# A four-phase graph network on one core: own term from DRAM, a wait for each half, and the last layer written node by node

## The reference, cut to what matters

```python
h = relu(layernorm(x1))                              # x1: the result of the first network, [3125, 128]
h3 = relu(mean(h[src] by dst) @ W_l0.T + b_l0 + h @ W_r0.T)      # third phase,  [3125, 256]
h4 = relu(mean(h3[src] by dst) @ W_l1.T + b_l1 + h3 @ W_r1.T)    # fourth phase, [3125, 256]
h5 = relu(h4 @ W_lin1.T + b_lin1)                                # [3125, 256]
out = x1 + h5 @ W_lin2.T + b_lin2                                # [3125, 128]
```

## Time and profile before

| what | value |
|---|---|
| time, median of 3 runs | 600.82 us (600.31 to 601.1) |
| profiled execution, its own time | 599.37 us |
| span of the profiled execution | 597.6 us |
| PE busy | 554.2 us, 93% of the span |
| PEld / DVE / ACT busy | 294.3 / 218.6 / 215.9 us |
| mean granted TensorE clock | 1.000 |
| DMA | 22.99 MB, mean 38 GB/s |

### The profile page before, as it was taken

How to read it: one execution, slowest core, us unless ns; L and a number is a source line. 1 busy time by engine, 2 the same in 40 slices (tenths; PEclk the granted TensorE clock), 3 DMA queues, 4 the chain that set the end, 5 groups by cost and what they waited for, 6 DMA issues and landing times.

```text
span 597.6 us, 9565 instructions
## 1 busy us (share of the span) xinstructions
PE 554.2 (93%) x3131; PEld 294.3 (49%) x3131; DVE 218.6 (37%) x489; ACT 215.9 (36%) x391; POOL 24.0 (4%) x34
## 2 busy tenths in 40 slices
PE   1457999999999999999999999999999999999996
PEld 0244655555554654445455555544544445454454
DVE  6888968577774227667311111100100001010000
ACT  1588857577674204454432212101101110111021
POOL 4320000000000000101100000000000000000000
PEclk9999999999999999999999999999999999999999
DMA  3700103010010133332110000200110202010011
GB/s 94 190 2 1 37 1 114 2 35 17 17 34 18 23 90 97 94 103 54 40 29 18 17 17 5 93 21 0 21 32 1 50 0 51 0 38 13 6 33 28
DMA packets 27421, 22.99 MB, mean 38 GB/s; under 512 B 4143, under 2 KB 26928, under 8 KB 27264
## 3 DMA queue, kind: packets, MB, share of 16 engines
q1 hardware_dynamic: 25670, 21.45, 13.5%
q10 hardware_dynamic: 1561, 0.84, 0.5%
q0 software_dynamic: 160, 0.33, 0.3%
HBM read 16.42 MB, written 6.19 MB: 38 GB/s over the span
## 4 chain that ended last, share of the span: by engine, by line
PE 86%; DVE 5%; ACT 3%; DMA 2%; issue 2%; POOL 1%; ACTq 0%; DVEq 0%; SPq 0%; POOLq 0%
PE ps L1011 53%; PE ps L1028 23%; PE ps L965 5%; PE ps L1021 2%; DVE hs_b L473 1%; DMA adj<-key_d,adj 1%; ACT hs_b L774 1%; PE ps L1245 1%; ACT adj L1481 1%; DMA invc<-inv_d 1%; POOL adj L1357 1%; PE ps L1217 1%; POOL adj L1364 1%; DVE adj L1408 1%; PE ps L1291 1%
## 5 line engine op out<-in xcount | busy, mean ns | idle before, releaser
L1011 PE MATMUL ps<-adj,hs_b 125*128 (+2 forms) x1050 | 205.7, 351 | 0.0
L1011 PE MATMUL ps<-adj,hs_a 125*128 (+2 forms) x700 | 158.6, 353 | 0.0
L1011 PEld LDWEIGHTS ps<-adj,hs_b 125*128 125x128 f16 x1050 | 95.9, 97 | 105.4 <-issue 9.9
L473 DVE TENSOR_TENSOR hs_b<-iota,hs_b 128x1024 f16<-128x1024 f16 x150 | 95.9, 686 | 29.6 <-PE ps L965 28.0
L965 PE MATMUL ps<-hs_b 128*128 128x125 f16 x625 | 69.4, 235 | 21.4 <-DVE hs_b L473 13.4
L813 ACT ACTIVATE adj<-ps 125x500 f32 (+2 forms) x150 | 80.2, 543 | 23.6 <-PE ps L965 17.3
L965 PEld LDWEIGHTS ps<-hs_b 128*128 128x128 f16 x625 | 46.7, 104 | 67.2 <-DVE hs_b L473 34.7
L1011 PEld LDWEIGHTS ps<-adj,hs_a 125*128 125x128 f16 x700 | 58.6, 98 | 38.8 <-issue 5.4
L763 DVE TENSOR_TENSOR hs_a<-ps,hs_a 125x512 f32<-125x512 f32 (+1 forms) x7 | 4.4, 634 | 170.3 <-PE ps L1291 170.3
L1028 PE MATMUL ps<-aggT,wts 128*128 128x500 f32 (+1 forms) x112 | 44.6, 540 | 0.4 <-ACT aggT L924 0.4
L1028 PE MATMUL ps<-aggT,hs_a 128*128 128x500 f32 (+1 forms) x84 | 35.1, 540 | 0.5 <-ACT aggT L952 0.5
(11 more groups left out here) (152 smaller groups left out, 358.8 us busy)
## 6 DMA issues: line engine op xcount, KB each, us to landing
invc<-inv_d SPq DMA_DIRECT2D x24, 250.0 KB, 3.3
self_d<-hs_b SPq DMA_DIRECT2D x6, 250.0 KB, 2.0
hs_b<-self_d SPq DMA_DIRECT2D x6, 250.0 KB, 3.5
hs_b<-in_x_dram SPq DMA_DIRECT2D x6, 250.0 KB
x_d<-hs_b SPq DMA_DIRECT2D x6, 250.0 KB
hs_a<-x_d SPq DMA_DIRECT2D x6, 250.0 KB
out_dram<-hs_a SPq DMA_DIRECT2D x6, 250.0 KB
wt_d<-adj SPq DMA_DIRECT2D x1, 1152.0 KB, 4.2
```

The source lines that it names most:

```text
L473: last = nc.vector.tensor_tensor(onehots[slot], iota2.unsqueeze(1).to_broadcast(shape), keys[:, ds(g * 4, 4), :].unsqueeze(2).to_broadcast ...
L1011: last = nc.tensor.matmul(acc[:, 0:n], hs[:, ds(s * (2 * w) + part * w + h * 128, 128)], adj[0:P, ds(c * (S * C) + s * n, n)], start=(isin ...
```

## The change

Three parts, all about the fourth phase.

1. SP stores each chunk's ReLU output of the third phase (`actT`) to a new DRAM tensor `h3_d` (f32, 500 KB for a full chunk), and ACT waits for that store before it overwrites `actT`. In the fourth phase SP loads `h3T` from it; `own4` and its two ACT copies are gone.
2. In `staged` TensorE waits in front of tile 0 and tile 25, each time for the eviction of the half whose bank it is about to overwrite. Phase 3 keeps the wait it had.
3. `lin2` takes slices of 125 nodes of `aggT` as the stationary operand and the weights (128 columns) as the moving one, and so writes node by feature into bank 2. `turn4` and ACT's bias copy are gone. VectorE adds the bias row (`bbb`, loaded once to all partitions, in the place of `zT`) to x1, and then writes the sum from bank 2.

```diff
+        h3_d = nc.dram_tensor("h3_d", [128, 2 * N], F32, kind="Internal").ap().rearrange("p (m n) -> p m n", m=2)
+        bbb = zT[:, 0:D]
...
                     load_inv("p3_", c + 1, nxt)
+                n = width(full)
+                sp.wait_ge(sem("p3_relu"), 2 * c + 2)
+                sp.dma_start(h3_d[:, :, ds(c * C, n)],
+                             actT.rearrange("p (m n) -> p m n", m=2)[:, :, 0:n]).then_inc(sem("p3_h3_out"), 16)
...
             load_x1(0, True)
+            sp.dma_start(bbb, bb.partition_broadcast(128)).then_inc(sem("p4_bb"), 16)
+
+            def load_h3(c, full):
+                n = width(full)
+                sp.dma_start(wts[:, 0:2 * C].rearrange("p (m n) -> p m n", m=2)[:, :, 0:n],
+                             h3_d[:, :, ds(c * C, n)]).then_inc(sem("p4_h3"), 16)
+            sp.wait_ge(sem("p3_h3_out"), 16 * NCH)
+            sp.wait_ge(sem("p3_h3"), 2 * NCH)
+            load_h3(0, True)
 
             def step4(c, full, nxt):
                 sp.wait_ge(sem("p4_agg_out"), 2 * c + 2)
                 if nxt is not None:
                     load_inv("p4_", c + 1, nxt)
+                    sp.wait_ge(sem("p4_h4"), 2 * c + 2)
+                    load_h3(c + 1, nxt)
                 sp.wait_ge(sem("p4_sum"), c + 1)
...
-                dve.wait_ge(sem("p4_turned"), c + 1)
                 dve.wait_ge(sem("p4_x1"), 16 * c + 16)
+                dve.wait_ge(sem("p4_bb"), 16)
+                nc.vector.tensor_tensor(tiles(x1in[:, 0:nt * D], D), tiles(x1in[:, 0:nt * D], D),
+                                        bbb[0:P].unsqueeze(1).to_broadcast([P, nt, D]), ALU.add).then_inc(sem("p4_x1b"), 1)
+                dve.wait_ge(sem("p4_lin2"), c + 1)
+                dve.wait_ge(sem("p4_x1b"), c + 1)
                 wait_past(dve, "p4_out", 16 * c)
-                nc.vector.tensor_tensor(outb[:, 0:nt * D], bank(3, nt * D, P), x1in[:, 0:nt * D], ALU.add).then_inc(
+                nc.vector.tensor_tensor(outb[:, 0:nt * D], bank(2, nt * D, P), x1in[:, 0:nt * D], ALU.add).then_inc(
                     sem("p4_sum"), 1)
...
                 wait_past(act, "p3_turned", 2 * c)
+                wait_past(act, "p3_h3_out", 16 * c)
...
-                for m in range(2):
-                    act.wait_ge(sem("p4_own"), 2 * c + m + 1)
-                    if m == 0:
-                        wait_past(act, "p4_turned", c)
-                    nc.scalar.activation(h3T[:, m * C:m * C + n], bank(2 + m, n), ACT.Copy).then_inc(sem("p4_ownT"), 1)
...
-                act.wait_ge(sem("p4_lin2"), c + 1)
-                nc.scalar.activation(h3T[:, 0:n], bank(2, n), ACT.Identity, bias=bbc).then_inc(sem("p4_lin2T"), 1)
...
-                        if at == 0 and ph > 2 and not done:
-                            wait_past(pe, f"p{ph}_agg_out", len(aggs) * c)
+                        if at % S == 0 and ph > 2 and at >= done:
+                            wait_past(pe, f"p{ph}_agg_out", len(aggs) * (c - 1) + at // S + 1)
...
-            def own4(c, full):
-                wait_past(pe, "p4_lin2T", c)
-                own(hbz, H, 0, 2, c, full).then_inc(sem("p4_own"), 1)
-                wait_past(pe, "p4_sum", c)
-                own(hbz, H, 1, 3, c, full).then_inc(sem("p4_own"), 1)
...
-                pe.wait_ge(sem("p4_ownT"), 2 * c + 2)
+                pe.wait_ge(sem("p4_h3"), 16 * c + 16)
...
-                dense(2, n, [(bv[:, k, :], aggT[:, k * C:k * C + n]) for k in range(2)]).then_inc(sem("p4_lin2"), 1)
-
-            def turn4(c, full):
-                pe.wait_ge(sem("p4_lin2T"), c + 1)
-                for t in range(width(full) // P):
-                    last = nc.tensor.transpose(bank(3, 4 * D, P)[:, t * D:(t + 1) * D], h3T[:, t * P:(t + 1) * P], identf[:])
-                last.then_inc(sem("p4_turned"), 1)
+                wait_past(pe, "p4_sum", c)
+                for t in range(n // P):
+                    for k in range(2):
+                        last = nc.tensor.matmul(bank(2, 4 * D, P)[:, t * D:(t + 1) * D], aggT[:, k * C + t * P:k * C + (t + 1) * P],
+                                                bv[:, k, :], start=(k == 0), stop=(k == 1))
+                last.then_inc(sem("p4_lin2"), 1)
             staged(4, [(fixed(0), hbz, H, 0), (fixed(1), hbz, H, 1)],
-                   [(0, own4, 1), (10, hidden4, 1), (20, lin1, 1), (30, lin2, 1), (40, turn4, 1)],
+                   [(10, hidden4, 1), (20, lin1, 1), (30, lin2, 1)],
```

More of the change, by code:

```diff
@@ L934, in act_layers @@
             chunks(act, step3)
-            h3T = wts[:, 0:2 * C]
             def step4(c, full):
                 n = width(full)
-                for m in range(2):
-                    act.wait_ge(sem("p4_own"), 2 * c + m + 1)
-                    if m == 0:
-                        wait_past(act, "p4_turned", c)
-                    nc.scalar.activation(h3T[:, m * C:m * C + n], bank(2 + m, n), ACT.Copy).then_inc(sem("p4_ownT"), 1)
                 for m in range(2):
@@ L1297, in pe_layers @@
             if not slow:
-                for part in (own4, hidden4, lin1, lin2, turn4):
+                for part in (hidden4, lin1, lin2):
                     part(NFULL, False)
```

## The result

The changed kernel takes 590.86 us, the median of 4 runs (590.59 to 592.12), against 600.57 us for the kernel before on the same chip: a ratio of 0.9846, 95% interval 0.9827 to 0.9866, which is 8.0 to 10.4 us less. The forecast was 591.8 us, with 590.0 to 594.6. A second series on another occasion gave 591.02 us and 0.9849 (0.9836 to 0.9863).

A forecast was written before the change was run, and what follows sets the result against it. TensorE was taken to bound the kernel, busy 554.2 of 597.6 us. Own term 5.28, waits 0.66, last layer 2.02 and end 1.10 summed to 9.06 us, so 600.82 became 591.8 us, range 590.0 to 594.6.

The forecast's parts named there:

- What bounds the kernel: Until the last aggregation ends, an edit's price is the TensorE time taken out or put in; afterwards every step's latency counts.
- Own term and the two waits: Fourth-phase passes: removing own4 gains 0.88 us x 6 = 5.28 us; waiting per half gains 0.06 + 4 x 0.15 = 0.66 us.
- the bare eviction: Start of each pass: removing own4 without the finer waits would expose the second bank's eviction, some 0.7 us a pass.
- A satisfied wait in mid-stream: A wait already met inside the TensorE stream: taken at nothing, bounded by 0.15 us once or twice a pass.
- The last layer: lin2 as 16 instructions takes 1.80 us against 2.12 with transposes; gain 0.32 us in passes 1 to 5, together 2.02 us.
- The rival with a slower pace: Short lin2 matmuls run at 0.146 us each, 2.34 us for 16; with two waits a pass, 596.8 us; chance 0.06.
- The rival of weight loads in series: lin2's f32 loads, 190 ns each, don't overlap: 4.8 us a layer, kernel 609.8 us; chance 0.04.
- After the last aggregation: End of the kernel: hidden4 starts 0.27 us earlier, bias copy and transpose going gives 0.83 us; together 1.10 us.
- The start of hidden4: After the last aggregation: hidden4 starts 0.10 us after VectorE's eviction, at 587.81 instead of 588.08 us; gain 0.27 us.
- The transfers: Added stores and loads, 500 KB each at 3.5 us, are covered and cost nothing; rival that they eat the gain: 0.02.
- The narrowest cover in the fourth phase: Last chunk: x1 lands by 591.0 us even at 4.4 us, and the final sum needs it at about 592.2.
- The sum: All terms: 5.28 + 0.66 + 2.02 + 1.10 = 9.06 us, giving 600.82 - 9.06 = 591.8 us.

The follow-up runs named there:

- e5: The kernel before with only the own term loaded from DRAM (old waits, old last layer): 600.00 us, ratio 0.9983 to 1.0001.
- e2: The changed kernel with the old last layer (500 columns, bias copy, transposes), so own term from DRAM and the two waits alone: 594.29 us.
- e3: The kernel before with only the two waits, at tile 0 and tile 25: 599.79 us, ratio 0.9984 to 1.0002.
- e4: The kernel before with only the last layer node by node, own4 waiting for the output sum before overwriting bank 2: 596.39 us.
- e6: The changed kernel with each last-layer matmul cut into two of 64 columns: 601.16 us, ratio 1.0009 to 1.0030.
- e1: The changed kernel with the old wait: TensorE waits in front of tile 0 until both halves are evicted; 596.84 us.
- e8: The changed kernel with hidden4's own-term matmuls first and its wait for the evicted sums behind them: 590.35 us.
- e7: The changed kernel with every store of the third phase made four times, to four tensors: 591.06 us.
- e9: The changed kernel with hidden4's own terms first and lin1's and lin2's waits split by ReLU half: 589.66 us, ratio 0.9827.

## Why the prediction was right, point by point

**What bounds the kernel** held for the change as a whole: PE's busy time fell from 554.2 to 545.3 us and the span from 597.6 to 588.7 us, 8.9 us each. As a rule for any single edit it doesn't hold. e5 took own4's 0.88 us out of each pass and the pass stayed at 34.34 us, because a wait came in their place; the forecast named that wait and priced the two edits together.

**Own term and the two waits** were priced at 0.88 and 0.15 us a pass. e2's pass is 34.34 - 33.31 = 1.03 us shorter, which is their sum. The claim that own4 hides the eviction, and that removing it alone would lay it bare, is the step that the runs test hardest. e5 gains 0.10 us, e3 0.73, both together (e2) 6.08. Some 5.3 us belong to neither part but to the pair. I had put the bare eviction at some 0.7 us a pass; it costs 1.0, as the hand-overs (0.15) and the late start behind it (0.16) come with it. The 0.66 us of the waits alone measured 0.73: the forecast had left out pass 6, where the 20 matmuls behind own4 went from 1.19 to 1.12 us. A satisfied wait in mid-stream, which I took at nothing with 0.15 us as its bound, costs nothing that e3 or the changed kernel shows.

**The last layer** was taken at 16 x 0.1125 = 1.80 us and is 1.75, between the bounds of 1.71 and 2.04. So a pass gains 0.37 and not 0.32 us, and pass 6, at 1.80 us, gains the 0.42 forecast: 2.27 us against 2.02. By e4, which also holds its share of the end, the part gives 3.11 us by itself, and by 9.19 - 6.08 also 3.11 on top of the other two. It is additive, since it meets neither the eviction nor the own term. The rival with a slower pace (2.34 us a chunk) is out: its 0.146 us held a start and a drain, as argued. The rival of weight loads in series is out by the 1.75 us themselves, and by e6. By the 81 ns a pair of the Trainium skill (TensorE: Matmul & The Clock Gate, Back-to-back issue gap), doubled for f32 as an estimate, the layer would take 2.6 us; the trace disagrees with that too.

**After the last aggregation** I had 1.10 us, and it is 6.36 - 5.40 = 0.96. ACT's copy and the transpose gave 0.84, with 0.83 forecast (5.67 us from hidden4's start to the sum before, 4.83 after). The start of hidden4 was mis-sized: I took 0.10 us from the eviction's end to TensorE, from the row of an ACT copy, and it is 0.25 (579.93 to 580.17). e1, e2 and e5 show the same 0.25 us there; at the start of a pass e1 and e5 show 0.13 us in the loop and 0.05 us in the written-out passes. Why the same hand-over from VectorE has three lengths, and why the last is more than the 0.10 us behind the ACT copy, isn't settled; that it goes away with the idle time is shown by e8.

**The transfers** cost nothing, as priced, though some landed later than my bounds: the fourth phase's weights in 5.8 us where I had 4.4, the x1 of the last chunk in some 5.2. The store took 3.1 us against the 3.5 assumed. e7 shows that the cover behind the ReLU is real. The narrowest cover in the fourth phase was the one that I named last. VectorE's add of the bias to the last chunk's x1 starts as soon as x1 is there:

```profile
583.66 0.29 DVE L780 TENSOR_TENSOR hs_a<-hs_a,zT 125x128 f32<-125x128 f32 x1 [3.74 <-DMA hs_a<-x_d]
```

It is done by 583.95 us, 1.05 us before the final sum; in e9 that is the wait that takes over.

**The sum.** 9.06 us forecast and 9.19 in the trace. That it is so close is in part luck: the last layer gave 0.25 us more than forecast and the end 0.14 us less, and the two offset. The medians moved 9.7 us, with 8.0 to 10.4 as their interval. The remaining 0.5 us aren't tied to a step; the third phase, 83.11 us before and after, holds none of them.

## What to carry to other kernels

Work that looks removable may be the cover of a wait: own4 cost 0.88 us a pass and hid nearly all of an eviction that stands bare for 0.84 us without it, so that its removal alone gave nothing and together with a finer wait gave 6 us. Before taking instructions off the engine that bounds a kernel, ask for the wait directly behind them, and when it would be satisfied. Where a chain ends the kernel, a wait for two things can be split, so that the matmuls that need only the first run ahead; look then at the transfer that lands next, as it will be the end.

## What the runs showed of the hardware

An f32 TensorE instruction with a weight load of its own takes 0.1075 us in a stream at 64 moving columns (e6) and 0.109 at 128, though the load is recorded with 190 ns. Below 128 columns narrower pieces gained nothing; the load is the likely cause, argued and not isolated. own4's f16 pairs with 125 columns ran at 0.055 us each. A load of 62.5 KB issued right behind a 250 KB store took 5.2 us (e9), and loads of 500 KB in the passes took 4.0 us by their median; whether the store is what held the small load up, no run separates. TensorE's start behind an awaited VectorE eviction came 0.05, 0.13 or 0.25 us later, by the place in the program.
